# Keeping the residual stream on chip and adding it with GpSimd in the last stage of a two-layer attention and mixture-of-experts kernel

## The reference

```python
x = x + _L0_xattn_ref(_layernorm(x), ctx, ctx, ...)   # mLSTM cell, 8 heads
x = x + _L0_ffn_ref(_layernorm(x), ...)               # 16 experts, each picks its tokens
x = x + _L1_xattn_ref(_layernorm(x), ctx)             # linear attention: Q + tril(K K^T) Q
x = x + _L1_ffn_ref(_layernorm(x), ...)               # 8 experts, two for each token
```

```
out = x + (t - mean(t)) * rsqrt(var(t) + 1e-5) * gamma + beta,   t = r + moe(r)
```

## Time and profile before

| what | value |
|---|---|
| median of three runs | 1300.97 us |
| profiled execution, own time | 1300.37 us |
| its span, first to last instruction | 1298.6 us |
| mean granted TensorE clock | 0.910 |
| busy TensorE, VectorE, ScalarE, GpSimd | 1131.4, 902.9, 790.0, 650.6 us |
| stage 3, first x load issued to last slot scatter landed | 677.5 to 799.3 us |
| stage 4, to the last scatter landed | 1257.62 us |
| stage 5 | 1257.62 to 1298.6 us |

### The profile page before, as it was taken

One profiled execution on the slowest core, in us unless ns is written; L12 is line 12 of the kernel. 1 busy time (PEld: TensorE's weight loads), 2 busy tenths in 40 slices (PEclk: granted clock), 3 DMA queues, 4 the chain that ended last, 5 costly groups with the idle time before them and its releaser, 6 DMA issues.

```text
span 1298.6 us, 23742 instructions
## 1 busy us (share of the span) xinstructions
PE 1131.4 (87%) x8184; PEld 1039.9 (80%) x8184; DVE 902.9 (70%) x1943; ACT 790.0 (61%) x1597; POOL 650.6 (50%) x581
## 2 busy tenths in 40 slices
PE   3789999998869999999988971999999999999950
PEld 2688787887858888888877861999999999999940
DVE  5677887676666666666637755787878787787847
ACT  3756566644235565565627640887878777787836
POOL 2435443443253666555443776255665745445326
PEclk8658999879999999999997865999999999999985
DMA  6544332221333778666647742568888776666649
GB/s 223 182 148 151 136 139 98 74 98 50 119 119 115 195 220 233 177 166 173 155 87 240 224 138 74 175 137 197 187 184 204 172 193 174 165 156 185 176 87 241
DMA packets 147497, 206.69 MB, mean 159 GB/s; under 512 B 29137, under 2 KB 121425, under 8 KB 140337
## 3 DMA queue, kind: packets, MB, share of 16 engines
q1 hardware_dynamic: 111376, 161.87, 38.1%
q0 software_dynamic: 35040, 42.75, 19.2%
q10 hardware_dynamic: 960, 0.54, 0.1%
HBM read 154.58 MB, written 50.53 MB: 158 GB/s over the span
## 4 chain that ended last, share of the span: by engine, by line
PE 70%; DVE 11%; ACT 6%; issue 5%; POOL 5%; DMA 2%; SPq 0%; ACTq 0%; DVEq 0%; POOLq 0%
PE quad L2029 14%; PE pb L2048 14%; PE quad L1200 13%; PE pb L1215 7%; PE quad L298 4%; PE pb L352 4%; PE pb L366 2%; POOL dSL L1882 2%; PE pb L264 1%; ACT Dm L839 1%; DVE Dm L527 1%; PE quad L2001 1%; PE quad L2023 1%; PE pb L1185 1%; PE quad L1480 1%
## 5 line engine op out<-in xcount | busy, mean ns | idle before, releaser
L2224 POOL DMA_INDIRECT dOUT<-y,es x71 | 118.9, 1675 | 192.4 <-DVE y L2130 179.5
L2048 PE MATMUL pb<-wh,hh 128*128 128x256 f32 x568 | 164.4, 289 | 1.1 <-DVE hl L2117 1.1
L2048 PE MATMUL pb<-wh,hl 128*128 128x256 f32 x568 | 160.7, 283 | 0.0
L2048 PE MATMUL pb<-wl,hh 128*128 128x256 f32 x568 | 160.6, 283 | 0.0
L1346 POOL DMA_INDIRECT dACC<-ye,idxJ x64 | 100.2, 1566 | 103.7 <-ACT ye L1310 54.7
L2186 ACT ACTIVATE gl<-quad,b1c 128x256 f32<-128x256 f32 (+1 forms) x312 | 124.6, 450 | 24.5 <-PE quad L2023 14.4
L2117 DVE TENSOR_TENSOR hl<-gl,hh 128x512 fp32r<-128x512 f32 (+1 forms) x156 | 99.6, 642 | 44.6 <-ACT hh L2191 42.5
L2029 PE MATMUL quad<-xh,wh 128*128 128x256 f32 x512 | 104.5, 286 | 8.2 <-ACT gl L2186 6.7
L2205 POOL DMA_INDIRECT xs<-dZ,es x71 | 95.9, 1351 | 28.0 <-issue 18.3
L2048 PEld LDWEIGHTS pb<-wh,hh 128*128 128x128 f32 x568 | 108.8, 192 | 1.3 <-DVE hl L2117 1.3
L2048 PEld LDWEIGHTS pb<-wl,hh 128*128 128x128 f32 x568 | 108.9, 192 | 0.0
(11 more groups left out here) (293 smaller groups left out, 3356.3 us busy)
## 6 DMA issues: line engine op xcount, KB each, us to landing
w2r<-in_W SPq DMA_DIRECT2D x39, 1024.0 KB, 5.8
MB<-dM SPq DMA_DIRECT2D x16, 1024.0 KB, 5.7
wraw<-in_Wg SPq DMA_DIRECT2D x16, 512.0 KB, 6.5
wraw<-in_Wu SPq DMA_DIRECT2D x16, 512.0 KB, 7.9
wraw<-in_Wd SPq DMA_DIRECT2D x16, 512.0 KB, 5.3
W<-in_W SPq DMA_DIRECT2D x8, 1024.0 KB, 10.7
w1p<-in_W SPq DMA_DIRECT2D x7, 1024.0 KB, 7.5
b2c<-in_b SPq DMA_DIRECT2D x39, 128.0 KB, 3.1
```

Of the source, the lines that this page charges most:

```text
L2048: ins = pe.matmul(bank.t[:, 0:256], a_[s][:, c, 128 * tt:128 * tt + 128], b_[n % 3][:, 256 * c:256 * c + 256], start=half == 0 and m == 0, ...
L2224: g.indirect_dma_start(out=dOUT[:, :], out_offset=bass.IndirectOffsetOnAxis(ap=es[i % 6][:, tt, 1:2].bitcast(U32), axis=0), in_=y1[i % 2][ ...
```

## The change

All eight pairs of x get a buffer of their own, `x2[0..7]`, that lives until the end. The store of x into `out` in stage 3, the accumulating beta transfers of stage 4 and the loads of `xc` are gone, and so is every accumulating store of stage 5. To make room, `w1p` has one buffer instead of two, and tiles of stage 4 are laid out in another order, with waits that go with it. In stage 5 VectorE first adds beta to all eight pairs of x (`add_beta`), ahead of its first wait for a load. GpSimd adds x to the blocks 0 to 13 (`BY_POOL`), VectorE to the blocks 14 and 15. All 16 blocks are stored plainly by SyncE, in their order. VectorE's new order is: statistics and shift of pairs 0 and 1; then for each j the statistics of pair j + 2, the two multiplies of pair j, the shift of pair j + 2, where the pairs 3 and 6 have their variance after the multiplies.

```diff
@@ stage 3 @@
+        x2 = M6.ring("x2", B // 2, [128, 4, D])
...
-        x2 = M4.ring("x2", 4, [128, 4, D])
...
             def x_in(j):
-                if j >= 4:
-                    sp.wait_ge(*x3_st[j % 4].of(j - 4))
-                    sp.wait_ge(*a_l1.of("z", 2 * j - 7))
-                sp.dma_start(x2[j % 4][:, :, :], by_chunk(dACC[pair_rows(j), :])).then_inc(*x2_ld[j % 4].up(j, by=16))
+                sp.dma_start(x2[j][:, :, :], by_chunk(dACC[pair_rows(j), :])).then_inc(*x2_ld[j].up(j, by=16))
...
                 if at(i) is not None:
-                    sp.wait_ge(*v_l1.of("x3", 2 * i + 1))
-                    sp.dma_start(by_chunk(out[pair_rows(i), :]), x2[i % 4][:, :, :]).then_inc(*x3_st[i % 4].up(i, by=16))
@@ stage 4 @@
-        w1p = M7.ring("w1p", 2, [128, 2, H1])
+        w1p = M7.sb("w1p", [128, 2, H1])
...
-            for s in (w1_ld, pad_st, *x3_st, *z_st):
+            for s in (w1_ld, pad_st, *z_st):
                 a.wait_ge(*s.all())
+            a.wait_ge(*pe_l1.of("Q", B - 1))
...
-                if i == 4:
-                    g.wait_ge(*ln_ld.all())
-                if 0 <= i - 4 < B:
-                    g.dma_start(by_chunk(out[rows(i - 4), :]), bet[:, :].unsqueeze(1).to_broadcast([128, 2, D]), accum_op=ALU.add
-                                ).then_inc(*beta_st.up(i - 4, by=16))
...
-                if j >= 2:
-                    sp.wait_ge(*pe_t.of("up", ORDER.index(ORDER[i] - 2), 1, 1))
...
+                if j:
+                    sp.wait_ge(*pe_t.of("up", ORDER.index(ORDER[i] - 1), 1, 1))
...
+            sp.wait_ge(*pad_st.all())
@@ stage 5 @@
+        BY_POOL = range(PAIRS - 1)
...
+            def add_beta(j):
+                v.tensor_tensor(x2[j][:, :, :], x2[j][:, :, :], bet[:, :].unsqueeze(1).to_broadcast([128, 4, D]),
+                                ALU.add).then_inc(*v_f.up("beta", j))
...
+            def weigh(j):
+                for b in (2 * j, 2 * j + 1):
+                    n = nc_[j % 4][:, chunks(b), :]
+                    v.wait_ge(*a_f.of("n", b))
+                    v.tensor_tensor(n, n, gam[:, :].unsqueeze(1).to_broadcast([128, 2, D]), ALU.mult).then_inc(*v_f.up("g", b))
+                    if j not in BY_POOL:
+                        v.wait_ge(*v_f.of("g", b))
+                        v.wait_ge(*v_f.of("beta", j))
+                        v.tensor_tensor(n, n, x2[j][:, chunks(b), :], ALU.add).then_inc(*v_f.up("y", b))
+
+            v.wait_ge(*ln_ld.all())
+            v.wait_ge(*a_l1.of("z", B - 1))
+            for j in range(PAIRS):
+                add_beta(j)
+            for j in range(2):
+                stats(j)
+                shift(j)
+            for j in range(PAIRS):
+                if j + 2 < PAIRS and j + 2 not in BY_ACT:
+                    stats(j + 2)
+                weigh(j)
+                if j + 2 in BY_ACT:
+                    variance(j + 2)
+                if j + 2 < PAIRS:
+                    shift(j + 2)
+                if j + 3 in BY_ACT:
+                    negative_mean(j + 3)
...
+            power(0)
+            power(1)
+            for j in range(PAIRS):
+                if j + 2 < PAIRS and j + 2 not in BY_ACT:
+                    power(j + 2)
+                for b in (2 * j, 2 * j + 1):
+                    if j in BY_POOL:
+                        n = nc_[j % 4][:, chunks(b), :]
+                        g.wait_ge(*v_f.of("g", b))
+                        g.tensor_tensor(n, n, x2[j][:, chunks(b), :], ALU.add).then_inc(*g_f.up("y", b))
+                    if b % 2 == 0 and j + 2 in BY_ACT:
+                        power(j + 2)
...
-            sp.wait_ge(*beta_st.all())
-            for b in range(ADDED, B):
-                sp.dma_start(xc[(b - ADDED) // 2][:, chunks(b), :], by_chunk(out[rows(b), :])).then_inc(*fx_ld[(b - ADDED) // 2].up(b, by=16))
...
+            for b in range(B):
+                sp.wait_ge(*(g_f if b // 2 in BY_POOL else v_f).of("y", b))
+                sp.dma_start(by_chunk(out[rows(b), :]), nc_[b // 2 % 4][:, chunks(b), :]).then_inc(*out_st[b % 8].up(b, by=16))
```

## The result

The changed kernel took 1309.31 us (median of seven runs, 1304.31 to 1312.18), the kernel before 1301.41 us beside it (1295.36 to 1303.27): ratio 1.0057, 95% interval 1.0037 to 1.0078. It lies inside the predicted range (1298.5 to 1309.5), by 0.2 us, and 4.3 us above the predicted 1305.0. It is slower by just over 0.5%, which I had put at 0.20.

The account below looks back on a forecast made before the run. The prediction took the final stage to be bound by GpSimd, the only full engine, with VectorE waiting for its powers. 1300.37 + 5.6 (final stage) - 1.0 (stage 4) + 0 (stage 3) = 1305.0 us; range 1298.5 to 1309.5.

Parts of the forecast that it names:

- the rival *slower: Final stage: ports held on every meeting, all 14 adds 1.73 and six powers 1.39, or power holds multiply; 1309.1 us, chance 0.17.
- What bounds the stage: Final stage: GpSimd is the only full engine, 9.91 of 10 us; VectorE waits for each power before the next shift.
- The beta adds: Start of final stage: eight VectorE adds, 1.15 us each, 9.2 in all, fit in the wait for loads at cost 0.
- The undisturbed GpSimd add: Final stage: each of GpSimd's 14 adds of 128x512 takes 1.29 us undisturbed, 18.1 us in all.
- Pair 2's variance: Final stage: ready at 1269.5, 0.9 us ahead of before; GpSimd's remaining work and waits are counted from there.
- the term for contention: Final stage: four powers +0.34 each, seven adds +0.38 each, VectorE's last pair late; stage +5.6 us instead of +0.5.
- The one-way rival: Final stage: only GpSimd is held, VectorE never; stage +2.5 us, 1301.9 us in all, chance 0.18.
- no contention: Final stage: no contention between VectorE and GpSimd that counts; stage +0.5 us, 1299.9 us in all, chance 0.14.
- Stage 4: Removing 16 beta transfers beside the matmuls saves 0.3 to 0.4 us in each of three short-visit periods; -1.0 us.
- Stage 3: Removing eight stores of x gains 0 us, since GpSimd's scatters set the pace; -1.1 as the end.
- The signs in the profile after: Adds near 1.29 and 1.67 us, multiply median well above 0.69, VectorE idle 2 us before shifts of pairs 3 and 6.
- the case that I forecast: Main case: final stage +5.6 us with holds in both directions, stage 4 -1.0, stage 3 0; 1305.0 us, chance 0.46.

Follow-up runs that it names:

- e1: Changed kernel with GpSimd waiting for VectorE's shift of pair j + 2 before its add; final stage 48.0 us, against 49.7 in the changed kernel.
- e4: Changed kernel with all adds of x on VectorE and only powers on GpSimd; final stage 44.4 us, against 49.7 in the changed kernel.
- e2: Changed kernel with gamma copied once to PSUM and read there by the 16 multiplies; final stage 45.3 us, against 49.7 in the changed kernel.
- e6: Changed kernel with the removed x stores of stage 3 and beta transfers of stage 4 put back, into an unread tensor; final stage 50.9 us.
- e5: The kernel before, unchanged, run again on another chip; final stage 40.4 us, against 41.0 in its first profile.
- e8: Changed kernel's final stage rewritten: no shift, gamma and intermediate tile in PSUM, ScalarE taking five pairs' statistics, four adds on GpSimd; ratio to the kernel before 0.9951.
- e11: Against e8: ten adds on GpSimd instead of four, ScalarE taking statistics of four pairs, new order, beta in PSUM; ratio to the kernel before 0.9978.
- e12: Against e11: ScalarE issues the odd loads of z instead of SyncE issuing all; ratio to the kernel before 0.9943.
- e10: Changed kernel with beta copied once to PSUM and read there by the eight beta adds; final stage 50.7 us.

## Why the prediction was right or wrong, point by point

- **The number was in part luck.** The measured median lies 0.2 us inside the top of the range, and that top was set by the rival *slower*, whose mechanism is not what happened.
- **What bounds the stage** was right: powers, shift and statistics in a ring between GpSimd and VectorE, with GpSimd the fullest.
- **The beta adds** were right: eight in 9.16 us, 1.15 each, and pair 0's variance was ready 5.02 us after the last scatter's landing, for 5.46 before. Only the scatter beside them was dearer than the 0.1 that I allowed in the range: 1.99 us for 1.55, 0.4 in all. A scatter slowed by the beta adds was one of my signs of being wrong, and it came.
- **The undisturbed GpSimd add** was right: 1.26 median where I took 1.29 from the earlier trace rows. The powers too: four of six at 1.38 to 1.39, two at 1.02.
- **Pair 2's variance** was to be ready 11.9 us after the landing and was at 11.6. From there to GpSimd's last add I had 30.3 us: adds 20.8, powers 7.7, waits 1.8. It took 33.4: adds 19.6, powers 7.6, waits 6.1. So the engine's own work was 1.3 us too high in the sum, and its waits for VectorE 4.3 too low. (The sum has 26.3 where 24.4 and 1.8 make 26.2; that changes nothing.)
- **The step that failed is the term for contention.** I counted it where I had rows, on GpSimd's adds (seven held, 2.7 us) and on VectorE's last pair (2.0 us). GpSimd's side came near: five adds held, 2.2 us, and four powers at 1.38 to 1.39. The other side did not: VectorE's instructions lose 13 us for the 2.0 counted. The largest part, 6.4 us, is the shift, which does not stand in my contention at all. I had thought of large tensors; the row of the add that was held says nothing of size, and a 128x4 instruction that starts just behind a 1.26 us add waits for its end like a large one. The order makes this certain: shift and add are both released by the same power. With shift and variance held my table gives 49.35 for the measured 49.7, and 45.6 without; the table is not shown, the measured counterparts are e1 to e4. That the hold is real is shown by e1 for the shift and by e2 for the multiply; for the variance only its times show it (see the end).
- **The one-way rival** (VectorE is never held, 1301.9) is refuted. So is *no contention*. The rival *slower* (1309.1) came nearest in time, and its heading, ports held on every meeting, is right in kind. But its terms were all 14 adds at 1.73 and six powers at 1.39, or a power that holds the multiply. Neither happened. In the timeline above the second of two multiplies that together take 1.28 lies in the power from 1264.55; so the earlier trace rows was read rightly. This also bounds the lock as the Trainium skill's page SBUF — State Buffer, section Who interferes with whom, states it: a VectorE instruction with two SBUF inputs contends with any GpSimd instruction that reads SBUF. For GpSimd's adds the runs agree, e2 above all (14.6 us against 10.3); for the power, which reads SBUF too, no multiply is held here. The meeting costs the power instead (1.38 for 1.02), so the two do contend; in which part of its time the power needs the way into SBUF no run shows.
- **Stage 4** (-1.0) was over-sized: 0.5 between the profiles of before and after (periods 56.04, 55.92 against 55.86, 55.65), 0.65 in e6, less 0.4 for the last scatter. **Stage 3** (0) can't be told from no change; and the 1.1 us that I took as its end held for that one trace only, since e5, the same kernel, has 8.9 us more in this stretch.
- **The signs in the profile after.** The adds do fall into two groups, 1.26 and 1.65 to 1.78. The gamma multiplies don't have the raised median that I foresaw: 12 of the 16 took 0.68 or 0.69 and four 1.74 to 1.76. VectorE idles 1.13 us ahead of the shifts of the pairs 3 and 6, where I had 2, as the hold of the variance fills part of that time.
- **The final stage and the medians.** With 8.7 for 5.6 and -0.5 for -1.0 the sum would have been 1308.6, for a measured 1309.31. The 0.20 for slower by over 0.5% was too low: the case that I forecast counted two holds of VectorE, and the one-way and no-contention rivals, 0.32 together, counted none.

## What to carry to other kernels

An engine's spare time isn't free when it shares a way into SBUF: before moving an elementwise operation from VectorE to GpSimd, list every VectorE instruction with two SBUF inputs, and every tensor_scalar on SBUF, that can start inside it. Look at the smallest first, since it waits for the rest of the add like a large one and stands on the path. Two cures worked. Moving the work back gave 44.4 us; moving one operand to PSUM gave 45.3, and 44.0 with the shift ahead of the adds. None of them beat the 41.0 of the kernel before. That took e8, e11 and e12, where gamma and the intermediate tile lie in PSUM and GpSimd's adds hold no large instruction of VectorE. Read a step's collisions from what releases it: shift and add were released by the same power and met six times out of six. And let GpSimd finish early: its closing step ended 4.3 us or more after its last operation and can end the kernel.

## What the runs showed of the hardware that I had not expected

- A scalar_tensor_tensor on 128x4 took 1.22 us, seven times its 0.17, whenever it started just after a GpSimd add of 128x512.
- A tensor_scalar on 128x4 with one SBUF input is held as well: 1.23 us twice in the changed kernel, 1.12, 0.52 and 0.42 in e11. Over the ten traces with adds on GpSimd, 37 such instructions began during an add. 23 of them ended 0.03 us after that add, so they took 0.24 to 1.23 us, depending on when they began. The other 14 took 0.16 or 0.17, and each of these had begun in the last 0.07 us of an add. The Trainium skill's page SBUF — State Buffer, section Who interferes with whom, says that tensor_scalar may take both ports when it runs in a faster mode; the 23 agree.
- Eight VectorE adds of 128x1024 with both inputs in SBUF slow the scatter that GpSimd issues beside them to 1.98 to 2.33 us, or 1.58 where it began late in an add; with one input in PSUM it is 1.55. The Trainium skill's page SBUF — State Buffer, section Who interferes with whom, has it, as an inference, that a tensor_tensor leaves the writing of descriptors alone; by e10 it doesn't, or another part of the scatter's issue needs the port.
- GpSimd's closing step ended 4.3 to 4.7 us after its last power or add in 13 of 14 traces and 5.5 in e6.
- A scalar_tensor_tensor of 128x256 costs VectorE 0.39 us where half a tensor_tensor of 128x512 costs 0.33.
